# The second layer's input turned by the DMA as two planes of two-byte halves

## The reference

```
x = layernorm(x + x @ (W0 * block_mask).T)
x = layernorm(x + x @ W1.T + b1 + lora(x))              # adapter chosen per sequence
x = layernorm(x + readout(4 blocks of scan and MLP on 128 channels))
x = layernorm(x + x @ W3.T + b3 + routed_lora(x))       # 8 experts, soft routing per sequence
```

## Time and profile before

| | |
|---|---|
| median of three runs | 1669.71 us (1665.78 to 1669.83) |
| profiled execution, its time | 1663.14 us |
| its span, first to last instruction | 1661.1 us |
| mean granted TensorE clock | 0.996 |
| TensorE busy | 1628.6 us (98%) |
| VectorE, ScalarE, GpSimd busy | 68%, 40%, 26% |
| transposes of `turn_x`, all layers | 512 |

### The profile page before, as it was taken

The page is one execution under the profiler, slowest core; times in us unless marked ns, Lnnn a source line. Parts: engine busy times, 40 slices in busy tenths (PEclk is TensorE's granted clock), DMA queues, the critical chain, the costliest instruction groups (busy, mean ns, idle before and its releaser), DMA issues.

```text
span 1661.1 us, 23126 instructions
## 1 busy us (share of the span) xinstructions
PE 1628.6 (98%) x7990; PEld 1316.5 (79%) x7990; DVE 1136.7 (68%) x2150; ACT 670.1 (40%) x987; POOL 428.3 (26%) x379
## 2 busy tenths in 40 slices
PE   8999999999999999999999999999899999999998
PEld 7888888888888888888866676666688788888886
DVE  6878886555655555566878777778867776776633
ACT  3645444533333333323345555545533333333311
POOL 4101010210000000000377777772213212221200
PEclk9999999999999999999999999999999999999999
DMA  7323323533333233331140000002546555555421
GB/s 280 114 102 140 114 103 139 181 117 118 111 109 115 104 118 112 144 119 64 42 162 26 1 1 1 1 14 96 208 146 219 195 190 190 187 198 186 135 81 51
DMA packets 73123, 196.59 MB, mean 118 GB/s; under 512 B 8882, under 2 KB 17074, under 8 KB 72754
## 3 DMA queue, kind: packets, MB, share of 16 engines
q1 hardware_dynamic: 52274, 125.92, 22.7%
q10 hardware_dynamic: 20736, 69.22, 10.5%
HBM read 122.75 MB, written 72.35 MB: 117 GB/s over the span
## 4 chain that ended last, share of the span: by engine, by line
PE 88%; DVE 5%; issue 3%; ACT 2%; DMA 1%; POOL 1%; SPq 0%; ACTq 0%; POOLq 0%; DVEq 0%
PE ps L854 16%; PE ps L856 16%; PE ps L855 16%; PE ps L1102 6%; PE ps L935 3%; PE ps L937 3%; PE ps L936 3%; PE ps L1044 3%; PE ps L868 3%; PE ps L1002 2%; PE ps L1050 2%; PE ps L1094 2%; PE ps L1092 2%; PE ps L1093 2%; PE ps L1070 1%
## 5 line engine op out<-in xcount | busy, mean ns | idle before, releaser
L854 PE MATMUL ps<-wall_x,x_hi 128*128 128x512 f32 x688 | 273.1, 397 | 5.4 <-ACT wall_x L1445 2.1
L2572 POOL TENSOR_TENSOR rstd<-var_eps,minus_half 128x1 f32<-128x1 f32 x96 | 62.8, 654 | 819.8 <-DVE minus_mean L1861 819.4
L856 PE MATMUL ps<-wall_x,x_lo 128*128 128x512 f32 x688 | 268.2, 390 | 0.0
L855 PE MATMUL ps<-wall_x,x_hi 128*128 128x512 f32 x688 | 268.1, 390 | 0.0
L854 PE MATMUL ps<-wall_y,x_hi 128*128 128x512 f32 x512 | 202.4, 395 | 0.0
L856 PE MATMUL ps<-wall_y,x_lo 128*128 128x512 f32 x512 | 199.6, 390 | 0.0
L855 PE MATMUL ps<-wall_y,x_hi 128*128 128x512 f32 x512 | 199.4, 389 | 0.0
L1793 DVE TENSOR_TENSOR row<-ps,bias 128x512 f32<-128x512 f32 x128 | 87.9, 687 | 105.8 <-PE ps L856 104.5
L854 PEld LDWEIGHTS ps<-wall_x,x_hi 128*128 128x128 f32 x688 | 129.2, 188 | 34.3 <-ACT wall_x L1445 3.9
L856 PEld LDWEIGHTS ps<-wall_x,x_lo 128*128 128x128 f32 x688 | 129.1, 188 | 27.7
L855 PEld LDWEIGHTS ps<-wall_x,x_hi 128*128 128x128 f32 x688 | 129.4, 188 | 25.1
(11 more groups left out here) (326 smaller groups left out, 3472.4 us busy)
## 6 DMA issues: line engine op xcount, KB each, us to landing
x_scratch<-row ACTq DMA_DIRECT2D x64, 512.0 KB, 2.7
x_in<-x_scratch SPq DMA_DIRECT2D x64, 512.0 KB, 4.0
out<-row ACTq DMA_DIRECT2D x32, 512.0 KB, 2.7
x_in<-in_x_t SPq DMA_DIRECT2D x29, 512.0 KB, 3.3
w_first<-in_w_t SPq DMA_DIRECT2D x56, 256.0 KB, 3.0
cx<-x_scratch SPq DMA_DIRECT2D x24, 512.0 KB, 4.2
x_scratch<-cx ACTq DMA_DIRECT2D x24, 512.0 KB, 2.9
w_more<-in_w_t SPq DMA_DIRECT2D x40, 256.0 KB, 3.2
```

Of the source, the lines that this page charges most:

```text
L854: pe.matmul(bank, hi[:, k], wall[:, k, 0, cols], start=(k == 0), stop=False)
L855: pe.matmul(bank, hi[:, k], wall[:, k, 1, cols], start=False, stop=False)
L856: return pe.matmul(bank, lo[:, k], wall[:, k, 0, cols], start=False, stop=(k == KC - 1))
L2572: pool.tensor_tensor(rstd[:, i:i + 1], var_eps[:, i:i + 1], minus_half[:, 0:1], ALU.pow)\
```

## The change

The second layer's input is turned on its way from DRAM. A transposing DMA takes two-byte elements, so ScalarE copies the normalised row of each first-layer tile into two planes, low and high halves of each float (`part_planes`, two activations of 1024 elements, then the store of both planes, 512 KB in all). SP issues two transposing DMAs for each tile, one a plane, into `x_planes`, and VectorE's `join_planes` copies the planes back to the interleaved halves of `x_in[1]`, where the splits read. `turn_x` stays for the last layer. `planes` and `x_planes` lie in memory that other tiles leave free, for which the load of `bias1` moves from `s = 10` to `s = 29`; `planes`, `x_planes` and `x_in[1]` have one place each. Waits for the row's store become waits for `normed`, which counts both activations of `part_planes` too. `load_x` of the second layer goes out two steps ahead in place of three.

```diff
-    x1 = scratch("x1_scratch", (TILES, P, D))
+    x1 = scratch("x1_scratch", (TILES, 2, P, D), U16)
+    planes = [at("planes_early", R + 18432, [P, 2, D], U16), at("planes_late", R + 12288, [P, 2, D], U16)]
+    x_planes = at("x_planes", FACTOR + 8192, [P, 2, KC, P], U16)
@@ sync: load_x
-                if s - 2 >= A_END:
-                    sp.wait_ge(x_turned, s - 1 - A_END)
+                if s - 2 >= B_END:
+                    sp.wait_ge(x_turned, turn_count(s - 2))
+                elif s == B_END + 1:
+                    sp.wait_ge(lo_ready, split_count(B_END - 1))
+                elif s > A_END:
+                    sp.wait_ge(x_turned, turn_count(s - 1))
...
-                    sp.dma_start(x_in[s % 2][:], x1[i]).then_inc(x_loaded[s % 2], 16)
+                    for part in range(2):
+                        sp.dma_start_transpose(x_planes[:, part], x1[i, part]).then_inc(x_loaded[0], 16)
@@ sync: first layer
-                if s != S_END:
+                if s != S_END and s + 3 < A_END:
                     load_x(s + 3)
...
+                if s == S_END + 2:
+                    for i in range(2):
+                        sp.wait_ge(stored[(S_END - 1 - i) % 2], 16 * ((S_END - 1 - i) // 2 + 1))
+                    sp.dma_start(bias1[:], a["bias1"].partition_broadcast(P)).then_inc(bias_loaded, 16)
+                if s + 2 >= A_END:
+                    load_x(s + 2)
@@ sync: second layer
-                if s + 3 < B_END:
-                    load_x(s + 3)
+                if s + 2 < B_END:
+                    load_x(s + 2)
@@ tensor
-                if s == A_END - 1:
-                    turn_x(A_END)
...
-                if s + 1 < B_END:
-                    turn_x(s + 1)
@@ scalar
+                if s >= A_END:
+                    act.wait_ge(normed, norm_count(s))
+                    act.dma_start(dense_out(s), row[:, i]).then_inc(stored[i], 16)
+
+            def part_planes(s):
+                i, out = s % 2, planes[s >= S_END]
+                act.wait_ge(normed, norm_count(s) - 2)
+                if s == 0:
+                    act.wait_ge(mm_done, mm_full(2))
+                else:
+                    act.wait_ge(stored[(s - 1) % 2], 16 * ((s - 1) // 2 + 1))
+                halves = row[:, i].bitcast(U16).rearrange("p (f h) -> p h f", h=2)
+                for part in range(2):
+                    act.activation(out[:, part], halves[:, part], ACT.Identity).then_inc(normed, 1)
+                act.wait_ge(normed, norm_count(s))
+                act.dma_start(x1[s].rearrange("h p f -> p h f"), out[:]).then_inc(stored[i], 16)
...
                 hold(p, 0)
+                if p > 0:
+                    part_planes(a - 2)
                 if more:
                     op_hi(p + 1, A11)
                 normalise(a - 1)
                 if more:
                     op_hi(p + 1, A12)
                 else:
                     split_x(S_END)
+                part_planes(a - 1)
                 hold(p, 1)
...
             normalise(S_END - 2)
+            part_planes(S_END - 2)
             take_a(0)
             for s in range(S_END, A_END):
                 split_x(s + 1)
...
                     if i == 1:
                         normalise(s - 1)
+                    if i == 2:
+                        part_planes(s - 1)
                 evacuate(s, 0)
...
                 normalise(s - 1)
+                if s == A_END:
+                    part_planes(s - 1)
@@ vector
+            def join_planes(s):
+                dve.wait_ge(x_loaded[0], 16 * x_loads(s))
+                dve.wait_ge(lo_ready, split_count(s - 1))
+                halves = x_in[1][:].bitcast(U16).rearrange("p (f h) -> p h f", h=2)
+                for part in range(2):
+                    dve.tensor_copy(halves[:, part], x_planes[:, part].rearrange("p k t -> p (k t)"))\
+                       .then_inc(x_turned, 1)
...
                 if s == A_END - 1:
                     choose(1)
+                if s + 2 >= A_END:
+                    join_planes(s + 2)
...
                 if i >= 1:
                     split_y(s - 1)
+                if s + 2 < B_END:
+                    join_planes(s + 2)
                 if b + 1 == BATCHES:
                     prepare(j)
```

More of the change, by code:

```diff
@@ L33 @@
 I32 = mybir.dt.int32
+U16 = mybir.dt.uint16
 ALU = mybir.AluOpType
@@ L138, in x_loads, with norm_count, turn_count @@
 def x_loads(s):
-    return (s - FIRST) // 2 + 1
+    if s < A_END:
+        return (s - FIRST) // 2 + 1
+    even, odd = x_loads(A_END - 2), x_loads(A_END - 1)
+    if s < B_END:
+        return even + 2 * (s - A_END + 1)
+    return (odd if s % 2 else even + 2 * TILES) + (s - B_END) // 2 + 1
+def norm_count(s):
+    return 3 * (s + 1) if s < A_END else 3 * A_END + s - A_END + 1
+def turn_count(s):
+    return 2 * (s - A_END + 1) if s < B_END else 2 * TILES + s - B_END + 1
 def before_in_slot(s):
@@ L707, in _ @@
                     sp.wait_ge(mm_done, mm_full(2))
-                    sp.dma_start(bias1[:], a["bias1"].partition_broadcast(P)).then_inc(bias_loaded, 16)
                     sp.dma_start(lora_in[:], a["lora_a"]).then_inc(lora_loaded, 16)
@@ L861, in turn_x @@
                 pe.wait_ge(lo_ready, split_count(s - 1))
-                if s == A_END:
-                    pe.wait_ge(evac_act, evac_count(A_END - 2, 1))
                 if s == B_END:
@@ L997, in turn_y @@
                 i = s - A_END
-                pe.wait_ge(normed, s + 1)
+                pe.wait_ge(normed, norm_count(s))
                 at_least(pe, y_hi_ready, i)
@@ L1334, in split_x @@
                 else:
-                    act.wait_ge(x_turned, s - A_END + 1)
-                    src = ps_x
+                    act.wait_ge(x_turned, turn_count(s))
+                    src = x_in[1][:] if s < B_END else ps_x
                 if s == B_END:
@@ L1376, in evacuate @@
                 act.wait_ge(mm_done, mm_count(s, half))
-                at_least(act, stored[s % 2], 16 * (s // 2))
+                if s >= 2:
+                    act.wait_ge(normed, norm_count(s - 2))
                 act.activation(row[:, s % 2, half * HALF:(half + 1) * HALF], ps[:, out_bank(s, half)], ACT.Identity)\
@@ L1389, in normalise @@
                    .then_inc(normed, 1)
-                act.wait_ge(normed, s + 1)
-                act.dma_start(dense_out(s), row[:, i]).then_inc(stored[i], 16)
+                if s >= A_END:
[13 more added lines that the diff above has]
+                act.dma_start(x1[s].rearrange("h p f -> p h f"), out[:]).then_inc(stored[i], 16)
             def take_a(chunk):
@@ L1566, in _ @@
             normalise(0)
+            part_planes(0)
             t_hi(2)
@@ L1569, in _ @@
             normalise(1)
+            part_planes(1)
             evacuate(2, 0)
@@ L1575, in _ @@
             normalise(2)
+            part_planes(2)
             evacuate(3, 1)
@@ L1580, in _ @@
             normalise(3)
+            part_planes(3)
             evacuate(4, 1)
@@ L1584, in _ @@
             normalise(4)
+            part_planes(4)
             evacuate(5, 0)
@@ L1589, in _ @@
             normalise(5)
+            part_planes(5)
             evacuate(6, 0)
@@ L1769, in split_x @@
             def split_x(s):
-                src = x_first[:, s] if s < FIRST else x_in[s % 2][:] if s < A_END else ps_x
+                src = x_first[:, s] if s < FIRST else x_in[s % 2 if s < A_END else 1][:] if s < B_END else ps_x
                 hi, lo = [flat(t) for t in x_parts(s)]
@@ L1791, in half_stats @@
                     dve.wait_ge(mm_done, mm_count(s, half))
-                    dve.wait_ge(stored[i], 16 * (s // 2))
+                    if s < A_END + 2:
+                        dve.wait_ge(normed, norm_count(s - 2))
+                    else:
+                        dve.wait_ge(stored[i], 16 * (s // 2))
                     dve.tensor_tensor(row[:, i, cols], ps[:, out_bank(s, half)], bias[:, cols], ALU.add)\
@@ L1844, in join @@
                 dve.wait_ge(evac_act, held_count(p, part))
-                dve.wait_ge(stored[s % 2], 16 * (s // 2))
+                dve.wait_ge(normed, norm_count(s - 2))
                 dve.tensor_tensor(row[:, s % 2, cols], ps[:, bank], held[:, part], ALU.add).then_inc(evac_dve, 1)
@@ L1897, in split_y @@
                 dve.wait_ge(y_hi_ready, i + 1)
+                if i == 0:
+                    dve.wait_ge(stored[(A_END - 1) % 2], 16 * (A_END // 2))
                 dve.tensor_tensor(y_lo[:, :, cols], ps_y.rearrange("p (k t) -> p k t", k=KC),
@@ L2570, in root @@
                 pool.wait_ge(ve_ready, 2 * s + 1)
-                at_least(pool, normed, s - 1)
+                if s >= 2:
+                    pool.wait_ge(normed, norm_count(s - 2) - (2 if s - 2 < A_END else 0))
                 pool.tensor_tensor(rstd[:, i:i + 1], var_eps[:, i:i + 1], minus_half[:, 0:1], ALU.pow)\
```

## The result

The changed kernel takes 1693.43 us (1692.24 to 1695.55, four runs) against 1669.77 us (1665.78 to 1669.90): ratio 1.0149, 95% interval [1.013, 1.0168]. Slower by 24 us, where 1662 was forecast. The profiled execution has a span of 1690.0 us against 1661.1, 28.9 us more. The medians are 23.7 us apart; the other 5 us belong to the executions that were profiled. The one before took 1663.14 us, less than any of its kernel's other runs on record, at a granted clock of 0.996, where thirty later ones had 0.989 to 0.996. The four of the changed kernel had 0.979 to 0.982.

A forecast was written before the change was run, and what follows sets the result against it. TensorE was taken as the bound, at least in layer two's first 24 tiles. Terms -22.4 + 5.3 + 5.3 + 2.0 + 0.3 + 0.1 + 1.5 = -7.9 us gave 1662 us on the 1669.71 median, range 1648 to 1682.

The forecast's parts named there:

- Transposes off TensorE, 0.90 per tile: Layer two on TensorE: eight transposes fewer per tile save 0.90 us, 22.4 us over tiles 33 to 57 plus 0.8.
- Transposing DMA hidden: Layer two loads: a tile's two transposing DMAs land within a 10.9 us window, so they cost nothing.
- Rival (a): Layer two: the transposing DMA does not keep up; at 16 us per tile's two, about 1777 us; chance 0.17.
- Joins 1.4 us, free in tiles 33 to 55: VectorE, layer two: a tile's two join copies take 1.4 us and fit a 2.2 us slack, nothing lost.
- Planes 1.05 us each: ScalarE, layer one: each part_planes activation costs as the 1.053 us f32 copy, 2.0 us a tile with overlap.
- Rival (b): ScalarE or VectorE dearer: joins 2.35 us or planes 1.245 us; within 2 us of before, or 1668 to 1676; chance 0.18.
- Paired tiles, +5.3 (0.65 a pair): Tiles 7 to 26: hold(p,1) starts 2.3 us later and ends 0.65 after TensorE wants it, in eight pairs: +5.3 us.
- The last pair, +0.1: Last pair of paired tiles: a longer split and two more picks in front of S1, so only +0.1 us.
- Last eight tiles, +5.3 of waits: End of layer two: joins ahead of prepare on VectorE delay six tiles by J less slack, +5.3 us.
- One of my six terms, -0.5: Last eight tiles: the tile with 1.9 us slack, J of 1.4 less its slack, counted as -0.5 us.
- `take_a(0)` +2.0: Behind part_planes(25) on ScalarE, where TensorE already waits for it (idle 0.70): +2.0 us in full.
- the turn +1.5: Turn to layer two: evacuate(31, 0) and choose(1) wait behind part_planes(30), delaying TensorE's pick_b: +1.5 us (0 to 4).

The follow-up runs named there:

- experiment 2: The changed kernel with a second place in memory for the planes of even tiles 12 to 24: 1676.34 us, ratio 1.0068.
- experiments 2 to 5: On the changed kernel: second planes place (1.0068); second part_planes behind hold(p,1), take_a(0) ahead of part_planes(25) (1.0011); joins of tiles 58 to 63 on ScalarE (1.0099); last two together (0.9951).
- Experiment 1: The changed kernel without the part_planes activations of tiles 7 to 26 and 28 to 31, stores kept: 1661.3 us, ratio 0.997.
- experiment 6: The changed kernel with reordered planes, last joins on ScalarE, and at the turn tile 32's load and join earlier, planes 26 to 30 later: 1655.14 us, ratio 0.9929.
- experiment 7: The kernel before the change, with three to six idle ScalarE activations planted ahead of hold(p,1) of pairs 2, 4, 6 and 8: 1684.97 us, ratio 1.0098.
- experiment 4: The changed kernel with join_planes of tiles 58 to 63 moved from VectorE to ScalarE, behind split_y: 1682.93 us, ratio 1.0099.

## Why the prediction was wrong, step by step

- **Transposes off TensorE, 0.90 per tile:** measured 19.6 / 23 = 0.85. Right; the credit was 1 us too large over those tiles.
- **Transposing DMA hidden:** right. 4.5 to 6.7 us for the pair against a window of 10.9, and tiles 33 to 55 run with TensorE full. Rival (a) did not come; the Trainium skill, Advanced Engine Details and Errata, section X-Bar Transpose (TRN2), calls these DMAs as fast as others. The trace agrees only roughly: 3.6 us for 256 KB, where a plain load of 256 KB takes 2.9 (`w_first`, both medians of the issues). The 5.9 us that I gave as the slowest load of 512 KB is a median; the slowest outside the start took 9.4 (`c_first`, at 839 us of the trace before). It did not matter here.
- **Joins 1.4 us, free in tiles 33 to 55:** right, and no wait of TensorE there.
- **Planes 1.05 us each:** right. Rival (b)'s dearer pieces did not come either.
- **Paired tiles, +5.3 (0.65 a pair):** here the forecast failed first. The step was "The second `part_planes` also waits for the first's store, issued at +5.4 and landed 2.7 later, before its turn at +8.4". That left 0.3 us of room, and I took the median of a trace in which those stores mostly ran alone: 42 of 64, while the other 22 took up to 4.4 us. In the change, over all 32 stores of planes, the five with no load by SP in flight took 2.80 to 2.84 us, the other 27 took 2.8 to 7.0. That the shared DMA engines cause it is argued from this, not tried. With the store in time the price of the order was right: in the pair of tile 15, `hold(p,1)` started 10.94 us after A11 (10.95) and TensorE waited 0.64 us, as in five pairs of experiment 2. But I took one pair for all eight. In the pairs of tiles 9, 17 and 21 the kernel before has less room, since `rstd` comes later: `hold(p,1)` starts 10.7, 10.4 and 10.1 us after A11 and not 8.65. In experiment 2 they wait 2.1, 2.0 and 1.3 us, which makes the 8.6. The first of them in the kernel before: the first matmul of A11, then ScalarE's wait and `hold(p,1)`:

```profile
112.55 0.39 PE L935 MATMUL ps<-wall_x,x_hi 128*128 128x512 f32 x1
...
120.70 0.30 ACT L1385 ACTIVATE shift<-minus_mean,rstd 128x1 f32<-128x1 f32 x1 [3.99 <-POOL rstd L2572]
...
123.27 0.58 ACT L1366 ACTIVATE held<-ps 128x512 f32<-128x512 f32 x1
```

- **The last pair, +0.1:** 7 us. SP's weight loads go out beside the store of tile 23, which takes 7.0 us; ScalarE stands 4.1 us in front of tile 24's planes and TensorE waits 4.9 for `b_rows`. I had looked at the length of the split there and not at what else moves bytes.
- **The clock, not in the sum at all:** paired tiles 27.1 us = 14.0 for `held` + 4.9 for `b_rows` + 1.5 for `x_lo` at the start + 5.3 for work at half clock (half of the 3.4, 3.2 and 4.0 us in which TensorE was busy in the three stretches) + 1.4, some 0.14 a wait, for restarts. In the last eight tiles it is 3.1 + 2.8 + 1.7 + 1.7 = 9.3 us at the four stretches. Taken over the execution, (1 - 0.979) x 1690.0 = 35 us of clock are missing, against 7 before (up to 18 in other executions of that kernel). I priced every wait at its own length.
- **Last eight tiles, +5.3 of waits:** the mechanism was right, and the size nearly: 8.0 - 1.2 = 6.8 us for row sums, 1.5 for `rstd` and 1.8 for `squares`, which I did not have. (One of my six terms, -0.5, counts a slack that is not used up as a gain.) The removed transposes of seven tiles give back 6, so that without the clock it is +4.1 where mine had +3.5. The clock's 9.3 make 13.4 of it, 2 more than the tally's 11.4; that rest was not traced.
- **`take_a(0)` +2.0 and the turn +1.5:** the first was right: TensorE waits 2.8 for `a_rows`, before 0.7. `choose` did not hold TensorE up in the change (in experiments 2 to 5 it did, for 1.4). The weight sums did, 2.2, which I had let cancel together with `join_planes(32)` against the removed wait (0.8). Two half-clock stretches add 3.1 and 1.7. Less a transposition and the removed wait that is 7.5 of the 9.0 from tile 25 to 32. Experiment 1 shows 5 us there with tile 27's planes alone, and experiment 6 takes more than half away by moving load, join and planes together; which of the three does how much was not tried apart.
- **Chances.** Slower than before had 0.26, all of it on a slow DMA and dearer pieces. The mechanism that came had no chance of its own: the wait chained through a buffer with one place was named in the working and put at nothing, and the clock was not named.

By the tally: -27 us for 32 tiles' transposes at 0.85, and 56 us lost. The paired tiles have 27 of these, the way to tile 32 10, the last eight 17, what follows 1 to 2.

## What to carry to other kernels

A new operation's price says little when it goes in front of one that another engine waits for: with the same work in another place in ScalarE's order, the ratio went from 1.0149 to 1.0011, 23 us. A buffer with one place turns a store's latency into a wait of the engine that fills it, and the latency to reckon with is the longest in traffic (7.0 us), not the median alone (2.7). On a kernel whose TensorE is full, the three longer waits of experiment 7 (2.6 to 5.0 us) cost 1.7 to 1.9 us more each for work at half clock. That belongs in the sum as a possible term, since waits of like length elsewhere cost nothing more. And one recurring stage read from one of its instances needs a look at the others: three of eight pairs had less room than the one I read.

## What the runs showed of the hardware

In experiment 7 the granted clock went to half for 3.4 or 6.8 us, 1.1 to 1.3 us after waits of 2.6 and 4.2 us or within one of 5.0, in a stream that is otherwise full. The length of the wait alone does not decide it. The 2.62 us ahead of 232.79 us in the change left the clock at full, the 2.56 us ahead of 185.21 in the planted kernel did not; behind 2.1 us (127.57) and 1.8 us (373.31) in the change it fell, behind 2.1 us (127.17) in experiment 2 it did not; and at 753.1 in the planted kernel it fell without a wait. The two-byte activations cost ScalarE as much as four-byte ones when they read every second half word and write densely (1.048 against 1.053 us for 1024 elements), and 1.36 us when they write every second half word (`x_in<-x_planes`, twelve on ScalarE in experiment 4); on VectorE the same strided copy is 0.745 us.
